# A graph-attention layer with a routed feed-forward: GpSimd's order, a projection in halves, overlapped tiles, and layer-norm sums on ScalarE

## The reference

```
h   = layernorm(x)                                        # "ln 1"
q, k, v = h Wq, h Wk, h Wv          (4 heads of 32)
s   = clip(q k^T / sqrt(32), -10, 10), and -10 where adj is 0
out = softmax(s) v Wo + bo + h
x   = x + layernorm(out) * gamma + beta                   # "ln 2"
g   = layernorm(x);  pair = the best 2 of 8 experts by g Wg + bg   # "ln 3"
x   = x + sum over the pair of  gelu(g W1 + b1) W2 + b2
```

## Time and profile before

| | |
|---|---|
| median of 3 runs | 852.67 us (850.55 to 852.83) |
| the profiled execution | 852.1 us, span 850.5 us |
| attention, first to last clip | 38.31 to 594.36 us |
| second stage | the rest of the span, 91 tiles |
| busy: PE, DVE, ACT, POOL | 722.9, 626.5, 491.2, 591.9 us |

### The profile page before, as it was taken

The page is one execution under the profiler, slowest core; times in us unless marked ns, Lnnn a source line. Parts: engine busy times, 40 slices in busy tenths (PEclk is TensorE's granted clock), DMA queues, the critical chain, the costliest instruction groups (busy, mean ns, idle before and its releaser), DMA issues. The chain is left out here.

```text
span 850.5 us, 17280 instructions
## 1 busy us (share of the span) xinstructions
PE 722.9 (85%) x5499; PEld 377.7 (44%) x5499; DVE 626.5 (74%) x1472; ACT 491.2 (58%) x873; POOL 591.9 (70%) x674
## 2 busy tenths in 40 slices
PE   2688998998989989899899898787577879999994
PEld 1222233232333333333323333231277768999994
DVE  2178898898988989889898898989774544455552
ACT  2456666766667666676665765635244535666662
POOL 4697665978779787797886977848764556445553
PEclk9989999999999999999999999998787989999998
DMA  7100000011010110101100001003211246432330
GB/s 260 62 1 25 14 13 13 13 39 50 14 39 13 39 50 13 39 13 39 50 13 26 14 27 37 14 26 110 76 54 57 68 133 189 123 85 85 102 93 1
DMA packets 45255, 45.43 MB, mean 53 GB/s; under 512 B 7413, under 2 KB 39424, under 8 KB 44720
## 3 DMA queue, kind: packets, MB, share of 16 engines
q1 hardware_dynamic: 38800, 30.00, 12.6%
q0 software_dynamic: 6368, 14.34, 4.8%
HBM read 31.46 MB, written 18.34 MB: 59 GB/s over the span
## 5 line engine op out<-in xcount | busy, mean ns | idle before, releaser
L641 ACT ACTIVATE e<-e 128x2048 f32<-128x2048 f32 x128 | 244.3, 1910 | 184.1 <-DVE e L783 181.3
L783 DVE SCALAR_TENSOR_TENSOR e<-scores_ps,bound_mem 128x2048 f32<-128x2048 f32 x128 | 291.9, 2281 | 43.8 <-PE scores_ps L393 42.4
L1189 POOL DMA_INDIRECT out<-e,near x91 | 90.3, 993 | 100.2 <-DVE e L964 51.7
L1167 POOL TENSOR_TENSOR ctx_part<-ctx_part,z_inv 128x1024 f32<-128x1024 f32 x62 | 119.8, 1933 | 49.1 <-DVE z_inv L799 49.1
L706 ACT ACTIVATE e<-scores_ps,bound_mem 128x128 f32<-128x128 f32 x364 | 103.8, 368 | 71.0 <-PE scores_ps L532 55.5
L412 PE MATMUL z_ps<-e,one_column 128*32 128x512 f32 x1024 | 137.4, 609 | 0.0
L1179 POOL TENSOR_TENSOR ctx_sum<-ctx_sum,ctx_part 128x512 f32<-128x512 f32 x90 | 115.8, 1287 | 6.0
L532 PE MATMUL scores_ps<-e,bound_mem 128*128 128x128 f32 x728 | 103.3, 287 | 13.7 <-DVE bound_mem L946 7.6
L532 PEld LDWEIGHTS scores_ps<-e,bound_mem 128*128 128x128 f32 x728 | 93.6, 201 | 17.4 <-issue 11.0
L946 DVE COPY bound_mem<-bound_mem 128x258 f32 x182 | 51.3, 324 | 55.6 <-issue 54.9
L791 DVE STREAM_TRANSPOSE ctx_part<-ctx_ps 128x512 f32<-128x512 f32 x128 | 90.1, 704 | 0.1
(11 more groups left out here) (156 smaller groups left out, 1046.7 us busy)
## 6 DMA issues: line engine op xcount, KB each, us to landing
near<-sorted_rows SPq DMA_DIRECT2D x91, 130.0 KB
near<-in_x SPq DMA_DIRECT2D x16, 256.0 KB
bound_mem<-in_adjT SPq DMA_DIRECT2D x4, 1024.0 KB, 11.0
x_post<-in_x SPq DMA_DIRECT2D x16, 256.0 KB, 2.7
sorted_rows<-sorted_rows SPq DMA_DIRECT2D x16, 130.0 KB
sorted_rows<-sorted_rows POOLq DMA_DIRECT2D x12, 130.0 KB
out<-e,near POOLq DMA_INDIRECT x91
sorted_rows<-x_rows,slot POOLq DMA_INDIRECT x64
```

What stands on the lines that cost most here:

```text
L641: nc.scalar.activation(every, every, ACT.Exp, scale=SCORE_SCALE).then_inc(exp_done, 1)
L783: dve.scalar_tensor_tensor(out=e[:, s % E_RING], in0=scores_ps[:], scalar=-CLIP, in1=to, op0=ALU.max, op1=ALU.min).then_inc(clipped, 1)
L1167: nc.gpsimd.tensor_tensor(pair, pair, z_inv[:, v % 2, j:j + 2].to_broadcast([P, 2, SQUARES, DH]), ALU.mult).then_inc(ctx_scaled, 1)
L1189: nc.gpsimd.indirect_dma_start(out=out_rows, out_offset=bass.IndirectOffsetOnAxis(ap=near_u[:, id_at:id_at + 1], axis=0), in_=e_flat[:, at ...
```

## The change

Five things are done, and nothing else in the computation.

1. ln 1's statistics leave DVE. ACT copies the block's four tiles with a running sum (`sum_x`, at j 1), makes minus the mean, and squares the centred tiles with a running sum (`square_x`, at j 4); POOL's `root_x` makes the variance, the root and the shift. `normalise_x` moves from j 7 to j 0 of the next pass.
2. POOL's order in a block becomes scale 0, add 1, scale 2, root ln 2, add 2, add 3, scale 4, residual, add 4, add 5, scale 6, root ln 3, add 6, add 7, root ln 1, scatter, beta. In the last block the scatter of block 12 comes right behind scale 0.
3. `project` is done in halves, two tiles at j 1 and two at j 2; `rank` moves from j 5 to j 6.
4. The last two contexts, turns, the last gate and choice of block 13 and block 14's projection move into slots 0 and 1 of the tile loop, and all jobs of the last blocks move three slots later. DVE reads a tile's offsets one slot ahead.
5. Pads: SP writes 12 (two beside each load from load 28 on), POOL 10, ACT 6, in slots from 22 on.

```diff
-SP_PADS = 16
-PAD_LOAD, PAD_SLOT = 19, 21
+SP_PADS, POOL_PADS = range(0, 12), range(12, 22)
+ACT_PADS = range(22, NP)
+PAD_LOAD, PAD_SLOT = 28, 22
...
+            def sum_x(v):
+                l = ln["1"]
+                act.wait_ge(x_loaded[v % 2], 16 * (v // 2 + 1))
+                need(act, xnT_filled, v - 1)
+                need(act, l["s_shift"], v)
+                for t in range(TILES):
+                    ins = nc.scalar.activation(xn[:, v % 2, t, :], x_in[:, v % 2, t, :], ACT.Copy,
+                                               accum_out=x_sum[:, t, :])
+                ins.then_inc(x_summed, 1)
+                act.wait_ge(x_summed, v + 1)
+                nc.scalar.activation(l["minus"][:, :, 0], x_sum[:, :, 0], ACT.Copy, scale=-1.0 / D)\
+                    .then_inc(l["s_minus"], 1)
+
+            def square_x(v):
+                l = ln["1"]
+                act.wait_ge(l["s_minus"], v + 1)
+                for t in range(TILES):
+                    ins = nc.scalar.activation(xn[:, v % 2, t, :], x_in[:, v % 2, t, :], ACT.Square,
+                                               bias=l["minus"][:, t, :], accum_out=x_square[:, t, :])
+                ins.then_inc(x_squared, 1)
...
-                    if j == 3 and is_block(u + 3):
-                        dve.wait_ge(x_loaded[(u + 3) % 2], 16 * ((u + 3) // 2 + 1))
-                        statistics(ln["1"], u + 3, x_in[:, (u + 3) % 2])
...
+            def root_x(v):
+                l = ln["1"]
+                pool.wait_ge(x_squared, v + 1)
+                need(pool, l["s_out"], v)
+                nc.gpsimd.tensor_scalar(l["var"][:], x_square[:], 1.0 / D, LN_EPS, ALU.mult, ALU.add)\
+                    .then_inc(l["s_var"], 1)
+                pool.wait_ge(l["s_var"], v + 1)
+                nc.gpsimd.tensor_tensor(l["rstd"][:], l["var"][:], minus_half[:], ALU.pow).then_inc(l["s_rstd"], 1)
+                pool.wait_ge(l["s_minus"], v + 1)
+                pool.wait_ge(l["s_rstd"], v + 1)
+                nc.gpsimd.tensor_tensor(l["shift"][:], l["minus"][:], l["rstd"][:], ALU.mult).then_inc(l["s_shift"], 1)
...
             for u in range(FIRST, BLOCKS):
+                last = u == BLOCKS - 1
                 if is_block(u - 1):
                     scale(u - 1, 0)
+                if last:
+                    scatter(u - 3)
+                if is_block(u - 1):
+                    add_context(u - 1, 1)
+                    scale(u - 1, 2)
                 if is_block(u - 2):
                     root(ln["2"], u - 2)
                 if is_block(u - 1):
-                    add_context(u - 1, 1)
-                    scale(u - 1, 2)
                     add_context(u - 1, 2)
+                    add_context(u - 1, 3)
+                    scale(u - 1, 4)
                 if is_block(u - 2):
                     add_residual(u - 2)
                 if is_block(u - 1):
-                    add_context(u - 1, 3)
-                    scale(u - 1, 4)
                     add_context(u - 1, 4)
+                    add_context(u - 1, 5)
+                    scale(u - 1, 6)
                 if is_block(u - 2):
                     root(ln["3"], u - 2)
...
-                    if j == (2 if last else 1) and is_block(u - 2):
-                        project(u - 2)
+                    if last and j == 2:
+                        project(13)
+                    if not last and j in (1, 2) and is_block(u - 2):
+                        project(u - 2, range(2 * j - 2, 2 * j))
...
+                if k < LAG:
+                    context(STEPS - LAG + k)
+                if k == 0:
+                    gate(13)
+                if k == 1:
+                    project(14)
```

More of the change, by code:

```diff
@@ L375, in _ @@
                     sp.wait_ge(pad_at_ready, 1)
-                if i >= PAD_LOAD and n_padded < SP_PADS:
-                    pad(n_padded)
-                    n_padded += 1
+                for k in SP_PADS[max(2 * (i - PAD_LOAD), 0):max(2 * (i - PAD_LOAD) + 2, 0)]:
+                    pad(k)
             for r in range(XT_RING):
@@ L475, in rank, with project @@
                           skip_group_check=True).then_inc(rank_filled, 1)
-            def project(v):
+            def project(v, tiles=range(TILES)):
                 pe.wait_ge(ctxT_ready, v + 1)
@@ L480, in project @@
                 pe.wait_ge(xnT_bo_ready, v + 1)
-                for t in range(TILES):
+                for t in tiles:
                     cols = slice(t * P, (t + 1) * P)
@@ L484, in project @@
                     ins = pe.matmul(job_ps[1][:, cols], xnT_bo[:, v % 4, cols], ident[:], start=False, stop=True)
-                ins.then_inc(proj_filled, 1)
+                if TILES - 1 in tiles:
+                    ins.then_inc(proj_filled, 1)
             def columns(g):
@@ L587, in _ @@
                         queries(u + 2)
-                    if j == (1 if last else 5) and is_block(u - 3):
+                    if j == (1 if last else 6) and is_block(u - 3):
                         rank(u - 3)
@@ L599, in _ @@
             for k in range(SLOTS):
[L600 removed]
+                if k == 4:
                     rank(13)
[L602 removed]
+                if k == 8:
                     project(15)
[L604 removed]
+                if k == 9:
                     turn_xn2(14)
[L606 removed]
+                if k == 11:
                     gate(14)
[L608 removed]
+                if k == 13:
                     rank(14)
[L610 removed]
+                if k == 15:
                     columns(1)
[L612 removed]
+                if k == 16:
                     turn_xn2(15)
                     ends(1)
[L615 removed]
+                if k == 17:
                     lookup(1)
[L617 removed]
+                if k == 18:
                     gate(15)
[L619 removed]
+                if k == 20:
                     rank(15)
[L621 to L626, removed]
+                if k in (22, 25):
+                    columns((k - 16) // 3)
+                if k in (23, 26):
+                    ends((k - 17) // 3)
+                if k in (24, 27):
+                    lookup((k - 18) // 3)
                 if k < FFN_TILES:
                     turn_tile(k)
+                if k < LAG:
[4 more added lines that the diff above has]
+                    project(14)
                 if k >= 2:
@@ L715, in _ @@
                         exponentials(s)
+                    if j == 0 and is_block(u + 2):
+                        normalise_x(u + 2)
+                    if j == 1 and is_block(u + 3):
+                        sum_x(u + 3)
                     if j == 2 and is_block(u + 2):
@@ L723, in _ @@
                         drain_v(u + 2)
+                    if j == 4 and is_block(u + 3):
+                        square_x(u + 3)
                     if j == 5 and is_block(u + 2):
@@ L1211, in _ @@
                 if is_block(u - 1):
-                    add_context(u - 1, 5)
-                    scale(u - 1, 6)
                     add_context(u - 1, 6)
@@ L1216, in _ @@
                 if is_block(u + 3):
-                    root(ln["1"], u + 3)
+                    root_x(u + 3)
                 if u == FIRST:
@@ L1226, in _ @@
                     ins.then_inc(gates_spread, 1)
-                if is_block(u - 3):
+                if is_block(u - 3) and not last:
                     scatter(u - 3)
```

142 lines of the change are left out of this document (81 added, 61 removed).

## The result

| | before | after |
|---|---|---|
| median (lowest to highest) | 852.75 us (850.55 to 854.79) | 824.14 us (822.60 to 825.48) |
| profiled execution: span | 850.5 us | 821.5 us |
| ratio of the times, 95% interval | | 0.9664 (0.9634 to 0.9695) |

The change takes 28.6 us off, where 16 were forecast (836 us, range 825 to 848).

A forecast was written before the change was run, and what follows sets the result against it. No engine is full; the largest wait named is DVE's for POOL's context sum, 27.7 us in 13 blocks. 852.1 - 17.6 (steady) + 4.0 + 7.6 (start) - 5.7 - 4.5 (tiles) = 835.9, said as 836 us; range 825 to 848.

The forecast's parts named there:

- Part 1: End of each block: POOL's new order ends DVE's wait for the context sum, 1.4 us a block, 18.2 us in 13.
- Part 2: Steady blocks, DVE: moving ln 1's statistics, rank and the projection's halves gains and costs nothing; up to 0.2 us each otherwise.
- Part 3: Steady blocks, ACT: sums and squares of 1.9 us each fit its idle time; cost 0.6 us in all.
- Rival (b): ACT overruns at j 1: sums take 3.0 us, costing 7.8 us in 13 blocks and 2 at the start; 846 us, chance 0.14.
- Rival (c): Square is not in exp's table, so ACT loads tables twice a block, 1.28 us each; 861 us, chance 0.05.
- Part 4: Start: the first clip comes 4.0 us later, and block 1 stalls on ln 1's root in POOL's queue, 7.6 us.
- Rival (a): The start costs little: read-out is free and block 1's stall is absorbed; 825 us, chance 0.14.
- ACT is free at 7.05, loads its table (1.28), sums (1.9), squares (1.9): Start, block 0: with POOL's root (1.6) this chain puts ln 1's norm at 13.8, 1.6 us later.
- Part 5: Tiles behind attention: earlier loads and first tiles save 5.7 us, spread pads 4.5 us.
- split into 5.7 and 4.5 us: Tiles: 5.7 us from three more tiles done early (1.9 us each), 4.5 us from the pads' new places.
- no transposes waiting for loads: Sign that the forecast is right: around the pads the transposes, which had waited 15.0 us for loads, no longer wait.
- Rival (d): The saved wait comes back: POOL and the tiles' tail with crowded pads give back 12 to 21 us; 848 to 857 us, 0.09.

The follow-up runs named there:

- e5: The changed kernel with the projection whole at j 1 again instead of in halves: 817.4 us, where the kernel before took 842.1 us.
- e1: The kernel before with POOL's new order alone, the last block's scatter staying where it was: 826.3 us, ratio 0.9685.
- e9: The changed kernel with POOL's old order, the last scatter kept early: 850.1 us, where the kernel before took 853.5 us.
- e2: The kernel before with the change of the tiles alone; order, statistics, projection and rank as before: 843.5 us, ratio 0.9879.
- e6: The changed kernel with rank back at j 5: 819.2 us, where the kernel before took 842.1 us.
- e3: The changed kernel with ln 1's statistics back on DVE at j 3, root and norm as before: 817.8 us, ratio 0.9587.
- e7: The changed kernel with ACT's four copies with a running sum of x done twice: 822.1 us, where the kernel before took 842.1 us.
- e8: The changed kernel with the pads' stores as before, 16 on SP, 12 on POOL, none on ACT: 825.6 us; kernel before 842.1 us.
- e12: The changed kernel with POOL's bounds for the first two blocks cut in three around ln 1's roots, run again: 817.2 us, ratio 0.9587.
- e10: The changed kernel itself run once more, on another chip: 822.9 us, ratio 0.9661 to the kernel before.
- e11: The kernel before run once more, unchanged, for its trace on another chip: 853.5 us.

## Why the prediction was wrong in size and right in kind

The mechanism of the largest part was right. Two terms of the sum failed: the steady gain, put at 17.6 us, measured 26.6, and the start, put at a cost of 4.0 us, measured 0.6. Where each went wrong follows.

**Part 1, 18.2 us for DVE's wait at j 7.** Right, and 1.7 us short: j 7 gave 20.9 us and j 0 took 1.0 back, 19.9. The chain "the sum is early, PE's scores are late next" is in the rows. In most blocks j 7 went from about 5.57 to 4.07 us, the 1.5 us of block 7; most of the shortfall is in blocks 2, 11, 13 and 14, where it was longer before (5.73 to 6.42).

**What it didn't have: the slow steps at j 1, 3.2 us** (three steps of 0.9, and 0.5 in block 2, which is the halves': 4.91 us in e5, 4.42 after). The forecast took block 7 as the pattern for all and so never met the three slow steps. PE's clock in the kernel before, at the end of block 7 and in block 8's first two steps, is the mean of 2.4 and 1.2 GHz stretches: 1.00, then 0.87 and 0.79.

```profile
305.10:310.70 5.60, 5.11 (x44) 1.41 (x36) 3.56 (x4) 4.54 (x7) 5.38 (x6) 1.00 0.01 3
310.70:315.50 4.80, 3.70 (x28) 1.66 (x28) 4.66 (x19) 3.45 (x5) 3.47 (x5) 0.87 0.32 80
315.50:320.80 5.30, 5.30 (x40) 2.65 (x36) 4.44 (x5) 1.91 (x1) 3.14 (x4) 0.79 0.21 78
```

(Columns: stretch, length, busy time of PE, weight loads, DVE, ACT and POOL, clock, DMA share, GB/s.) What PE did before: it waited 1.10 us for DVE's clip, which the late sum had pushed back. In e1 the same scores follow the gate without a wait, and the clock stays at 1.00. PE before, then PE and the stretch in e1:

```profile
310.81 1.08 PE L454 MATMUL job_ps<-wg_sb,xn2T 128*128 128x35 f32 x8
312.99 1.14 PE L393 MATMUL scores_ps<-near 32*128 32x512 f32 x8 [1.10 <-DVE e L783]
```

```profile
303.63 1.08 PE L454 MATMUL job_ps<-wg_sb,xn2T 128*128 128x35 f32 x8
304.64 1.14 PE L393 MATMUL scores_ps<-near 32*128 32x512 f32 x8
```

```profile
306.80:311.20 4.40, 4.40 (x40) 2.46 (x36) 4.37 (x5) 1.91 (x1) 2.02 (x2) 1.00 0.21 79
```

That the order ends the slow steps is shown by e1. e9, with the old order in the changed kernel, bears it out in part: PE waits 1.12 to 1.64 us for the clip at j 0 of blocks 3 to 14 again, and the clock falls again in three of them, but the step at j 1 then takes 4.42 to 4.48 us, not 5.33, and that at j 2 up to 4.45 instead of 4.15. e9's first two steps of block 8:

```profile
317.26:322.06 4.80, 3.33 (x24) 1.43 (x27) 4.66 (x18) 2.52 (x3) 3.47 (x5) 0.83 0.15 55
322.06:326.50 4.44, 4.44 (x32) 1.63 (x28) 4.41 (x6) 3.06 (x7) 2.58 (x3) 0.80 0.40 121
```

So one fall of the clock costs 0.9 us in the kernel before and 0.3 to 0.4 in e9; that the halved projection, which leaves PE less work at j 1, makes the difference is argued, not shown. That the clock falls through PE's wait is argued too. For it: in the three kernels with this wait (before, e2, e9) the clock falls in three of the twelve blocks that have it, in the kernels without it in none of blocks 2 to 14. Against: block 7 of the kernel before has the same wait and keeps its clock.

**Part 2, at nothing.** The failed step is that the statistics and rank were put at nothing, because their work looked covered: the change's gain at j 2 to j 6 together is 3.5 us (0.2 of it, at j 2, comes with the order, as e1 shows). Rank's move gives 2.1 us by the sum of all steps (e6) and 2.4 at j 5 alone, the statistics 1.0 by the sum (e3) and 1.3 at j 3 and j 4. That PE's chain doesn't contain the statistics is only half of it: without the statistics j 3 falls from 4.2 to 3.6 or 3.7 us, so they did set that step, and j 4 rises from 3.6 to 4.0, where PE's chain takes over. The halves are at nothing but for block 2, as forecast (e5).

**Part 3, 0.6 us for ACT.** The sums came out at 1.5 us instead of 1.9 and the squares at 1.65; e7 shows that even twice the sums cost nothing in the steady part. Rival (b), in which ACT overruns at j 1, falls with it. Rival (c), table loads in the steady part, falls with the trace: there is one load before the gelus, at 4.09 us. The Trainium skill, page "ScalarE: Activation LUTs", section "Table sets: the hidden batching unit", names a few functions as in every set, and square is not among them. It does not say that exp's set lacks square, as the strict reading of the forecast took it; in this trace copy, square, identity and exp run from the one load.

**Part 4, the start.** Block 1's stall is the forecast step for step: 7.3 us for 7.6 (the forecast's own terms, 96.6 less 88.9, give 7.7), ACT's wait 8.24 for 8.3, and from the norm to the scores 8.8 us for 9.6. Rival (a), in which it is absorbed, was wrong here and right on the other half: the start itself cost 0.6 us and not 4.0. The failed step is "ACT is free at 7.05, loads its table (1.28), sums (1.9), squares (1.9)": the load is hidden in a wait of ACT for a transfer, which the new first instruction has and the old one had not (the 7.05 of the earlier trace rows is PE's wait for that transfer; ACT starts at 6.92), sums and squares are 0.6 us less, and POOL's root takes 1.96 us instead of 1.6. The norm of block 0 so starts at 12.08 us and not at 13.8, 1.7 of the 3.4 us. The other 1.7 are the later sums, reckoned at 0.7 and 0.8, and the squares, at 0.9: the sum of block 1 runs beside PE's transposition and ends with it, so that the drain starts at 15.04, before at 15.07. Only what goes beyond (all of e7's second sums) delays the drain. How the 1.7 us divide between the sums and the squares was not measured.

```profile
13.63 0.29 ACT L669 ACTIVATE near<-near 128x128 f32<-128x128 f32 x1
...
13.78 1.12 PE L424 MATMUL job_ps<-ident,near 128*128 128x128 f32 x4 [6.19 <-ACT near L659]
...
14.93 0.21 ACT L673 ACTIVATE ln_minus<-x_sum 128x4 f32<-128x4 f32 x1
15.04 0.58 ACT L696 ACTIVATE near<-job_ps 128x512 f32<-128x512 f32 x1
```

**Part 5, the tiles.** 10.4 us for 10.2. The tiles' own edits give 8.9 us behind the last clip (e2), and POOL's order may give some of the rest: 2.6 and 2.7 us by the traces of e1 and e9, no more than two traces of the kernel before differ by. So the close agreement is partly luck. The loads start where the forecast put them: 594 less the 18.1 us by which the last clip is earlier is 575.9, and they start at 575.56. The pads' share isn't settled by e8 (8 us on its chip, 2 at the least), so the forecast's split into 5.7 and 4.5 us is not tested. The sign "no transposes waiting for loads" came nearly true in the first trace (2.1 us) and not on the quicker chip (10.7 in e5).

**The sum.** Steady part 26.6 for 17.6 (1.7 at j 7 and j 0, 3.2 at j 1, 3.5 at j 2 to j 6, 0.6 for ACT: the 9.0 that are missing), start 0.6 for 4.0, tiles 10.4 for 10.2: 852.1 - 26.6 + 0.6 + 7.3 + 0.7 - 10.4 = 823.7, against the profiled 823.5. The two large errors went the same way: the gain was reckoned from one block and the costs of the start were taken without cover. Rival (d), by which the tail gives the saved wait back, falls with the 10.4 us. The range's low end took in rival (a) and no larger steady gain.

## What to carry to other kernels

Where one engine's queue mixes a job with a deadline and jobs that wait for others, put the jobs that wait behind those that don't: that alone was worth 27 us here (e1), and all the other parts together 3.4 (e9), since the tiles' 10 us are nearly eaten up by the 7 us that blocks 0 and 1 take longer. Read a wait's price from all blocks, not from one: steps of the same code differ where the wait moves TensorE's clock. When a job goes into a queue earlier than its input is ready, look at what stands behind it in the start, where nothing is in flight yet; filling that wait with independent work won another 5.8 us (e12 beside e10).

## What was not expected of the hardware

A running sum on ScalarE costs a second instruction, the read-out of 0.19 us, which overlaps in part: copies of 128x128 with it start 0.295 us apart. TensorE's granted clock fell to a mean of 0.79 to 0.84 over a step that followed a wait of only 1.09 to 1.28 us, in 3 of the 12 blocks that all have such waits (1.06 to 1.31 us), and in the same three in two executions (the kernel before and e11). In the kernels whose blocks have no such wait it never fell in blocks 2 to 14. That the wait is the cause is argued, not shown.
